# Attention passes of a graph network: each tile weighted right behind its scores, and each link of the scan chain in a turn of its own

## The chip, the core and the metric

The program runs on one NeuronCore of a Trainium2 chip. Its engines are TensorE (PE; its weight loads are listed apart as PEld), VectorE (DVE), ScalarE (ACT), GpSimd (POOL) and SyncE (SP). Each has its own queue of instructions, works it off in order, and meets the others through semaphores. The metric is the device time of one execution in microseconds, lower is better.

## The reference

Four layers of a graph network on 3125 nodes of 256 features. Each layer has a graph part, a mixing part over all nodes and an MLP or a mixture of experts. Three of the graph parts and the gate of one mixture are attention over edges: for each edge a score per head from its source and target node, a softmax over the edges that end in the same node, and the weighted sum of the sources' values. The first layer's:

```python
scores = jnp.einsum('ehd,ehd->eh', Q[dst], K[src]) * SCALE
attn_max = jnp.zeros((n, H), scores.dtype).at[dst].max(scores)
w = jnp.exp(scores - attn_max[dst])
attn_sum = jnp.zeros((n, H), w.dtype).at[dst].add(w)
w = w / (attn_sum[dst] + 1e-08)
msg = V[src] * w[:, :, None]
out = jnp.zeros((n, H, D), msg.dtype).at[dst].add(msg)
```

The third layer builds each edge's message from two rows with the edge's two attributes; the gate of the first mixture and the fourth layer add a number of the source to one of the target, and send the sum through a leaky ReLU. All of it is float32.

## The kernel before, in words

Edges are sorted by target node. A row of an edge tile holds up to 8 edges (SLOTS = 8) of one target, a tile has NP = 125 rows. `edge_pass` (L502) goes over the G tiles of a pass. It runs four times: "ae" (kind "dot", 8 heads, 125 tiles, a ring of 4 row buffers, of which one lies in `net_X`), "be" ("add", 4 heads, 91 tiles, ring of 8, the experts' matmuls as `inner`), "ee" ("mix", 4 heads, 125 tiles, ring of 5, a mixing part as `beside`) and "ge" ("add", 8 heads, 125 tiles, ring of 5, nothing beside). For each tile g:

- POOL gathers 8 x 125 rows of the sources' table from HBM by indirect DMAs (L581), one for each slot, into place g mod RING of the ring. For the first slot it waits until the tile RING places back has been used: slot_summed of TensorE, in ee (for every slot) message_ready of DVE.
- ACT makes a one-hot matrix of the rows' targets (`one_hot`, L679, L681). TensorE turns it (`turn`, L608), ACT copies the turned one out of PSUM (`turned_copy`, L689), and TensorE looks up the target's own vector with it (`own`, L617). These three are missing in ee.
- DVE computes the scores (`score`, L740 to L768), the largest score of each row (`top`), and the scores less it (`below`). ACT takes the exponential (`weigh`, L695). DVE weights the gathered values with it (`send`, L778 in ee, L781 elsewhere) and sums the weights (L784).
- TensorE sums the 8 slots into PSUM with an identity matrix (`sum_slots`, L627). ACT copies the sum out (`keep`, L703).
- Every 4 tiles (a block b) follows the scan chain, which finds each node's maximum across rows: TensorE transposes the block's tops (`flip`, L638), DVE scans them forth and back (`scan`, L791, L796), TensorE transposes the result back (`flip_back`, L644, L645), DVE takes the differences (`fall_behind`, L809), ACT their exponentials (`factors`, L712 to L714), and DVE lowers what has been gathered so far (`lower`, L816).
- DVE scales the kept sum by its factor (`scale`, L824), TensorE adds the rows of one node together with the one-hot matrix (`total`, L652), and DVE adds that to the accumulator (`add`, L830).

The order on each engine is written out by hand: each engine runs a loop over turns i, and in a turn does one step for each of several tiles, as for DVE `score(i + 1)`, `send(i)`, `scale(i - 6)`, `add(i - 7)`. PSUM holds two tiles of sums: `sum_slots(g)` waits for `keep` of g - 2. There is one buffer for the weights (`weigh(g)` waits for `send(g - 1)`) and one for the totals (`total(g)` waits for `add(g - 1)`).

`sum_pass` (L856), between be and ee, gathers tiles in the same way with a ring of 4, but has no scores: TensorE sums the slots as they arrive.

## Time and profile before

| | |
|---|---|
| median of 3 runs | 12751.7 us (12729.91 to 12787.16) |
| profiled execution, span | 12797.9 us, mean granted TensorE clock 0.722 |
| TensorE matmul busy | 7767.2 us, 61% |
| VectorE busy | 6057.8 us, 47% |
| GpSimd busy | 6028.7 us, 47% |
| ScalarE busy | 2346.5 us, 18% |
| gathers and scatters of GpSimd | 621.62 MB, 22.6% of the 16 DMA engines' time |

No time of the profiled execution is known but its span from the first to the last instruction; it is 46 us above the median of the runs. Busy is the time in which an engine has an instruction under way. The idle time of an engine is listed with what ended it: "issue" when the profile shows nothing that it waited for, "remote" when a semaphore ended it whose sender the profile doesn't name. Semaphores are used again by later stages, so a releaser's name can be that of another stage.

### The profile page before, as it was taken

The numbers are of one execution on the slowest core, as the hardware profiler recorded it, in microseconds if no ns is written. First come the engines' busy times: TensorE is split into PE (matmuls) and PEld (weight loads), VectorE is DVE, ScalarE is ACT, GpSimd is POOL, SyncE is SP. The second block draws the span as 40 slices with busy tenths as digits, with TensorE's granted clock in tenths as the row PEclk, the third lists the DMA queues.
The fourth block names the chain that finished last, engine by engine and source line by source line (L and its number), as shares of the span: only waits on it lengthen the run. The fifth ranks groups of instructions, "written<-read, shape, count | busy, mean of one in ns | idle before, by whom it ended". The sixth has DMA issues, their size and how long they took to land. (4 is left out here: it accounts for less than half of the span.)

```text
span 12797.9 us, 114013 instructions
## 1 busy us (share of the span) xinstructions
PE 7767.2 (61%) x32472; PEld 6013.2 (47%) x32472; DVE 6057.8 (47%) x17050; ACT 2346.5 (18%) x5596; POOL 6028.7 (47%) x6164
## 2 busy tenths in 40 slices
PE   4555365256665468844777675676646846666546
PEld 3433344245554367743566433455535635554334
DVE  6556565378886322222122144665551134444455
ACT  0111001011110134420122011133311211111001
POOL 0666546566663066614666504665521136666000
PEclk9655555577777677767788786777768967777777
DMA  1212122166665111222333601121343323336200
GB/s 46 60 58 61 42 75 65 46 175 184 183 183 111 27 17 19 19 52 80 92 91 92 77 7 47 45 45 42 40 43 101 105 58 96 95 95 90 32 4 22
DMA packets 478286, 903.72 MB, mean 71 GB/s; under 512 B 173139, under 2 KB 290029, under 8 KB 476915
## 3 DMA queue, kind: packets, MB, share of 16 engines
q0 software_dynamic: 277568, 621.62, 22.6%
q1 hardware_dynamic: 200106, 274.86, 6.7%
q8 instruction: 271, 4.44, 0.1%
q14 instruction: 341, 2.79, 0.1%
HBM read 827.17 MB, written 68.88 MB: 70 GB/s over the span
## 5 line engine op out<-in xcount | busy, mean ns | idle before, releaser
L581 POOL DMA_INDIRECT ee_rows<-e_table,net_mr_data x1000 | 999.7, 1000 | 1097.9 <-POOLq L1725 468.0
L581 POOL DMA_INDIRECT ge_rows<-g_table,net_mr_data x1000 | 961.0, 961 | 654.0 <-issue 285.7
L913 POOL DMA_INDIRECT ce_rows<-c_table,net_mr_data x1000 | 947.7, 948 | 501.0 <-issue 246.0
L402 POOL DMA_INDIRECT main_slots<-em_load,em_where x784 | 807.8, 1030 | 690.1 <-DVE em_where L376 439.3
L581 POOL DMA_INDIRECT ae_rows<-a_table,net_mr_data x752 | 719.2, 956 | 431.9 <-issue 216.4
L581 POOL DMA_INDIRECT be_rows<-b_table,bx_br_data x728 | 696.3, 957 | 454.9 <-issue 196.6
L627 PE MATMUL ee_to_act<-ee_message,net_eye 125*125 125x256 f32 x2000 | 599.0, 447 | 211.9 <-issue 208.3
L627 PE MATMUL ge_to_act<-ge_rows,net_eye 125*125 125x256 f32 x2000 | 633.7, 470 | 153.6 <-issue 145.7
L402 POOL DMA_INDIRECT gat_slots<-eg_load,eg_where x512 | 528.9, 1033 | 392.2 <-DVE eg_where L376 227.7
L936 PE MATMUL ce_part_ps<-ce_rows,net_eye 125*125 125x256 f32 x2000 | 577.2, 435 | 217.7 <-issue 111.5
L359 PE MATMUL em_look_ps<-em_table,em_hot_tT 25*128 25x125 f32 x1568 | 332.3, 391 | 565.9 <-issue 467.8
L627 PEld LDWEIGHTS ge_to_act<-ge_rows,net_eye 125*125 125x125 f32 x2000 | 466.2, 238 | 289.3 <-issue 201.1
L627 PEld LDWEIGHTS ee_to_act<-ee_message,net_eye 125*125 125x125 f32 x2000 | 439.4, 224 | 340.5 <-issue 266.0
L936 PEld LDWEIGHTS ce_part_ps<-ce_rows,net_eye 125*125 125x125 f32 x2000 | 425.3, 216 | 352.8 <-issue 180.0
L359 PEld LDWEIGHTS em_look_ps<-em_table,em_hot_tT 25*128 25x128 f32 x1568 | 307.6, 296 | 587.4 <-issue 497.2
L1101 DVE TENSOR_TENSOR c_acc<-c_acc,ce_total_ps 125x512 f32 x125 | 85.8, 686 | 858.6 <-remote 468.8
L359 PE MATMUL eg_look_ps<-eg_table,eg_hot_tT 25*128 25x125 f32 x1024 | 239.6, 421 | 387.1 <-issue 308.2
L652 PE MATMUL ae_total_ps<-ae_part,ae_hot 125*125 125x264 f32 x500 | 206.9, 554 | 400.8 <-issue 241.2
L2279 PE MATMUL be_own_h_bank<-bx_XT,bx_w 128*128 128x125 f32 x1600 | 311.9, 353 | 188.7 <-issue 114.0
L627 PE MATMUL ae_to_act<-ae_rows,net_eye 125*125 125x256 f32 x1504 | 412.2, 436 | 16.3 <-ACT ae_hotT L689 7.9
L359 PEld LDWEIGHTS eg_look_ps<-eg_table,eg_hot_tT 25*128 25x128 f32 x1024 | 222.9, 325 | 403.8 <-issue 383.0
L778 DVE TENSOR_TENSOR ee_message<-ee_rows,ee_weight 125x512 f32<-125x512 f32 x500 | 309.4, 680 | 181.8 <-remote 167.1
(1006 smaller groups left out, 18274.5 us busy)
## 6 DMA issues: line engine op xcount, KB each, us to landing
em_key_row<-main_keys SPq DMA_DIRECT2D x98, 512.0 KB
f_w<-in_L_ffn_W_dram SPq DMA_DIRECT2D x40, 1024.0 KB, 11.8
eg_key_row<-gat_keys SPq DMA_DIRECT2D x64, 512.0 KB
ce_rows<-c_table,net_mr_data POOLq DMA_INDIRECT x1000
ee_rows<-e_table,net_mr_data POOLq DMA_INDIRECT x1000
ge_rows<-g_table,net_mr_data POOLq DMA_INDIRECT x1000
main_slots<-em_load,em_where POOLq DMA_INDIRECT x784
b_own_rows<-bx_kept SPq DMA_DIRECT2D x100, 125.0 KB
```

The costliest lines, as they stand in the source:

```text
L359: ins = pe.matmul(look_ps[i % 2][:, u, 0:NP], hot_tT[:, i % 2, u * 128:(u + 1) * 128], table[:, i % 2, u, 0:NP], start=True, stop=True)
L402: pool.indirect_dma_start(edge["slots"], bass.IndirectOffsetOnAxis(ap=where[:, c:c + 1], axis=0), load[:, c, :], None).then_inc(scattered, 16)
L581: pool.indirect_dma_start(rows[n][:, s, :], None, table, bass.IndirectOffsetOnAxis(ap=data[:, g, s, 0:1].bitcast(I32), axis=0)).then_inc(g ...
L627: ins = pe.matmul(part_ps(g), const["eye"][0:NP, 0:NP], values(g)[:, s, :], start=(s == 0), stop=(s == SLOTS - 1))
L652: ins = pe.matmul(total_ps[0:NP, q, 0:WA], hot[0:NP, g % HOTS, q * NP:(q + 1) * NP], part[0:NP, g % PARTS, :], start=True, stop=True)
L778: ins = dve.tensor_tensor(message[0:NP, n, :, h * dv:(h + 1) * dv], r[0:NP, :, 0:dv], w[:, :, h:h + 1].to_broadcast([NP, SLOTS, dv]), ALU. ...
L913: pool.indirect_dma_start(rows[:, g % RING, s, :], None, table, bass.IndirectOffsetOnAxis(ap=data[:, g, s, 0:1].bitcast(I32), axis=0)).the ...
L936: pe.matmul(part_ps[g % 2][0:NP, 0:D], const["eye"][0:NP, 0:NP], rows[0:NP, g % RING, s, :], start=(s == 0), stop=(s == SLOTS - 1)).then_i ...
L1101: dve.tensor_tensor(at, at, total_ps[g % 2][0:NP, :, :], ALU.add).then_inc(added, 1)
L2279: ins = pe.matmul(self.h_bank[:, m * NP:(m + 1) * NP], self.w1[:, e, q, m * 128:(m + 1) * 128], self.XT[:, q, t * NP:(t + 1) * NP], start= ...
```

## The change

Only the order inside `edge_pass` is changed. On DVE a turn is now `score(i)`, `scale(i - 6)`, `send(i)`, `add(i - 7)`, `scan`; on TensorE `flip`, `flip_back`, `total(i - 7)`, `sum_slots(i)`, `turn(i + 4)`, `own(i + 2)`; on ACT `weigh(i)`, `keep(i - 1)`, `turned_copy(i + 3)`, `factors`, `one_hot(i + 5)`. The scan chain of block b is flip and scan in turn 4b + 4 (3 before), flip_back and fall_behind in 4b + 5 (4 and 5 before), lower in 4b + 7 (6 before). The waits that order the use of PSUM follow the new distances. The lines of the kernel from L834 on move down by one.

```diff
@@ def sum_slots(g) on TensorE
-                    if QW and g + 4 < G:
-                        pe.wait_ge(turned_sb, g + 5)
+                    if QW and g + 2 < G:
+                        pe.wait_ge(turned_sb, g + 3)
@@ TensorE's loop
-                for i in range(-5, G + 8):
+                for i in range(-6, G + 8):
+                    for b in range(BLOCKS):
+                        if i == b * BLOCK + 4:
+                            flip(b)
+                        if i == b * BLOCK + 5:
+                            flip_back(b)
                     if 0 <= i - 7 < G:
                         total(i - 7)
-                    for b in range(BLOCKS):
-                        if i == b * BLOCK + 3:
-                            flip(b)
-                        if i == b * BLOCK + 4:
-                            flip_back(b)
-                    if 0 <= i - 1 < G:
-                        sum_slots(i - 1)
-                    if QW and 0 <= i + 5 < G:
-                        turn(i + 5)
-                    if QW and 0 <= i + 3 < G:
-                        own(i + 3)
+                    if 0 <= i < G:
+                        sum_slots(i)
+                    if QW and 0 <= i + 4 < G:
+                        turn(i + 4)
+                    if QW and 0 <= i + 2 < G:
+                        own(i + 2)
@@ def turned_copy(g), def keep(g) on ACT
-                    if 0 <= g - 6 < G:
-                        act.wait_ge(slot_summed, g - 5)
+                    if 0 <= g - 4 < G:
+                        act.wait_ge(slot_summed, g - 3)
...
-                    if QW and g + 6 < G:
-                        act.wait_ge(turned, g + 7)
+                    if QW and g + 4 < G:
+                        act.wait_ge(turned, g + 5)
@@ ACT's loop
-                    if 0 <= i + 1 < G:
-                        weigh(i + 1)
-                    if QW and 0 <= i + 4 < G:
-                        turned_copy(i + 4)
-                    if 0 <= i - 2 < G:
-                        keep(i - 2)
+                    if 0 <= i < G:
+                        weigh(i)
+                    if 0 <= i - 1 < G:
+                        keep(i - 1)
+                    if QW and 0 <= i + 3 < G:
+                        turned_copy(i + 3)
...
-                    if 0 <= i + 6 < G:
-                        one_hot(i + 6)
+                    if 0 <= i + 5 < G:
+                        one_hot(i + 5)
                     if beside is not None:
-                        beside.scalar(act, i)
+                        beside.scalar(act, i - 1)
                     if inner is not None:
-                        inner.scalar(act, i)
+                        inner.scalar(act, i - 1)
@@ DVE's loop
-                    if 0 <= i + 1 < G:
-                        score(i + 1)
                     if 0 <= i < G:
-                        send(i)
+                        score(i)
...
                     if 0 <= i - 6 < G:
                         scale(i - 6)
+                    if 0 <= i < G:
+                        send(i)
+                    for b in range(BLOCKS):
+                        if i == b * BLOCK + 7:
+                            lower(b)
                     if 0 <= i - 7 < G:
                         add(i - 7)
                     for b in range(BLOCKS):
-                        if i == b * BLOCK + 6:
-                            lower(b)
-                        if i == b * BLOCK + 3:
+                        if i == b * BLOCK + 4:
                             scan(b)
```

DVE in ge, a turn that ends with a scan, before (the names are tiles and buffers; `ge_below` is what ACT's exponential reads, `ge_weight` what it writes):

```order
L749 TENSOR_TENSOR ge_term<-ge_rows,ge_own_ps 125x64
L760 SCALAR_TENSOR_TENSOR ge_raised<-ge_term 125x64
L762 TENSOR_TENSOR ge_raised<-ge_raised,net_mr_data 125x64
L764 TENSOR_REDUCE ge_row_top<-ge_raised 125x8
L766 TENSOR_SCALAR ge_top<-ge_row_top 125x8
L768 TENSOR_TENSOR ge_below<-ge_raised,ge_top 125x64
L781 TENSOR_TENSOR ge_rows<-ge_rows,ge_weight 125x8x256
L784 TENSOR_REDUCE ge_part<-ge_weight 125x8
L824 TENSOR_TENSOR ge_part<-ge_part,ge_factor 125x264
```

and now:

```order
L749 TENSOR_TENSOR ge_term<-ge_rows,ge_own_ps 125x64
L760 SCALAR_TENSOR_TENSOR ge_raised<-ge_term 125x64
L762 TENSOR_TENSOR ge_raised<-ge_raised,net_mr_data 125x64
L764 TENSOR_REDUCE ge_row_top<-ge_raised 125x8
L766 TENSOR_SCALAR ge_top<-ge_row_top 125x8
L768 TENSOR_TENSOR ge_below<-ge_raised,ge_top 125x64
L824 TENSOR_TENSOR ge_part<-ge_part,ge_factor 125x264
L781 TENSOR_TENSOR ge_rows<-ge_rows,ge_weight 125x8x256
L784 TENSOR_REDUCE ge_part<-ge_weight 125x8
```

In the first piece the rows up to L768 are of tile i + 1 and L781, L784 of tile i; in the second both are of tile i. `scale` (L824) has gone in between.

TensorE in ge, around the turn with the flip, before (L652 is `total`, L638 `flip`, L627 `sum_slots`, L608 `turn`, L617 `own`):

```order
L617 MATMUL ge_own_ps<-g_s,ge_hotT 125x8
L652 MATMUL ge_total_ps<-ge_part,ge_hot 125x272 x2
L638 MATMUL ge_topT_ps<-net_eye,ge_top 8x125 x4
L627 MATMUL ge_to_act<-ge_rows,net_eye 125x256 x8
L608 MATMUL ge_to_act<-net_eye,ge_hot 125x125 x2
```

and now:

```order
L617 MATMUL ge_own_ps<-g_s,ge_hotT 125x8
L638 MATMUL ge_topT_ps<-net_eye,ge_top 8x125 x4
L652 MATMUL ge_total_ps<-ge_part,ge_hot 125x272 x2
L627 MATMUL ge_to_act<-ge_rows,net_eye 125x256 x8
L608 MATMUL ge_to_act<-net_eye,ge_hot 125x125 x2
```

The flip has gone ahead of the total. The sum is of tile i - 1 in the first piece and of tile i in the second, the turned tile i + 5 and i + 4, the looked-up tile i + 3 and i + 2.

## Rows read from the trace of the kernel before

**Rows 1.** Busy time of each stretch; columns as in its first line:

```profile
core 0: us, PE busy (x) PEld busy (x) DVE busy (x) ACT busy (x) POOL busy (x), PEclk, DMA share, GB/s
2573.00:4079.00 1506.00, 996.60 (x3563) 770.16 (x3564) 1209.80 (x1506) 220.38 (x690) 954.97 (x1000) 0.78 0.65 175
4450.00:5586.00 1136.00, 888.89 (x4909) 803.45 (x4910) 275.43 (x1182) 496.75 (x1164) 696.33 (x728) 0.73 0.17 19
...
7770.00:9443.00 1673.00, 1130.50 (x4212) 806.48 (x4213) 971.45 (x2307) 474.42 (x1140) 999.74 (x1000) 0.76 0.28 44
10436.00:11937.00 1501.00, 950.66 (x3564) 744.14 (x3564) 699.60 (x1507) 247.01 (x815) 960.99 (x1000) 0.73 0.43 91
```

**Rows 2.** POOL's waits by pass: engine, line, releaser, us in total, times, longest:

```profile
POOL ae_rows L581 <- remote: 116.1, 37, 5.5
POOL net_X L581 <- remote: 55.4, 17, 4.0
...
POOL be_rows L581 <- remote: 158.4, 81, 2.9
...
POOL ce_rows L913 <- remote: 124.0, 71, 4.5
POOL ce_rows L913 <- PE ce_part_ps L936: 114.2, 129, 4.4
...
POOL ee_rows L581 <- DVE ee_part L784: 333.5, 44, 14.9
...
POOL ge_rows L581 <- remote: 183.1, 60, 4.6
```

**Rows 3.** DVE's waits in ae, ge and ee:

```profile
DVE ae_rows L740 <- DMA ae_rows<-a_table,net_mr_data: 94.2, 41, 13.0
...
DVE a_acc L830 <- remote: 18.3, 13, 2.9
...
DVE g_acc L830 <- DMA eg_src_i<-in_gat_src_dram: 463.5, 90, 11.5
...
DVE ge_upto L791 <- remote: 86.8, 27, 5.3
...
DVE e_acc L830 <- remote: 339.8, 30, 21.6
```

**Rows 4.** Timeline of ge: start, us, engine, line, operation, count, [idle before, releaser]:

```profile
11031.21 0.50 PE L617 MATMUL ge_own_ps<-g_s,ge_hotT 125*125 x4
...
11034.32 1.79 PE L652 MATMUL ge_total_ps<-ge_part,ge_hot 125*125 125x272 f32 x4 [2.61 <-DVE g_acc L830]
...
11035.91 2.98 PE L627 MATMUL ge_to_act<-ge_rows,net_eye 125*125 125x256 f32 x8
...
11040.96 0.95 POOL L581 DMA_INDIRECT ge_rows<-g_table,net_mr_data  x1 [0.30 <-issue]
...
11044.59 1.87 PE L627 MATMUL ge_to_act<-ge_rows,net_eye 125*125 125x256 f32 x4 [1.51 <-issue]
...
11044.88 0.37 ACT L689 COPY ge_hotT<-ge_to_act 125x250 f32<-125x250 f32 x1 [6.30 <-remote]
11044.94 0.94 POOL L581 DMA_INDIRECT ge_rows<-g_table,net_mr_data  x1 [3.03 <-remote]
11044.97 0.72 DVE L830 TENSOR_TENSOR g_acc<-g_acc,ge_total_ps 125x544 f32 x1 [6.38 <-DMA eg_src_i<-in_gat_src_dram]
```

**Rows 5.** Timeline of ee, DVE and POOL:

```profile
8723.59 0.70 DVE L830 TENSOR_TENSOR e_acc<-e_acc,ee_total_ps 125x528 f32 x1 [16.18 <-remote]
...
8732.09 0.94 POOL L581 DMA_INDIRECT ee_rows<-e_table,net_mr_data  x1 [12.62 <-DVE ee_part L784]
```

**Rows 6.** Instructions on ge_rows: line, engine, count, ns min/median/max, first and last start:

```profile
L581 POOL DMA_INDIRECT ge_rows<-g_table,net_mr_data x1000: 940/946/1812, 10436.7 to 11872.0; - x167
...
L781 DVE TENSOR_TENSOR ge_rows<-ge_rows,ge_weight x125: 2269/2280/2289, 10459.9 to 11909.2; 125x2048 f32<-125x2048 f32 x125
```

**Rows 7.** Groups of ee from 7900 to 9300: count, busy us, mean ns, idle before:

```profile
L695 ACT ACT_TABLE_LOAD x46 | 59.0, 1283 | 73.2 <-issue 53.1 <-DVE ee_part L784 19.8
```

## The prediction

> **What bounds the kernel now.** I read the busy times by stretch first, then who waited for whom in each stretch, then a few microseconds of the timeline. The change touches only edge_pass, so the question is what holds its four runs: "ae" (2573 to 4079), "be" (4450 to 5586), "ee" (7770 to 9443) and "ge" (10436 to 11937), together 1506 + 1136 + 1673 + 1501 = 5816 us. The reader should see that no engine fills any of them: in ge TensorE's matmuls are busy 951 us of 1501, DVE 700, GpSimd (POOL) 961; in ae DVE 1210 of 1506 [rows 1]. The stretch 5870 to 7350 is sum_pass, which the diff leaves alone.
>
> A tile is 8 gathers of POOL. Where POOL is free to go on they start 1.25 us apart, 0.95 busy and 0.30 "issue" [rows 4], so 10.0 us a tile is a floor. The 1000 gathers of ge start over 1435.3 us, 11.5 us a tile [rows 6]; ae, with as many and a pass as long, is taken for the same [rows 1]. What lies between is POOL's wait for a free row buffer: 116.1 + 55.4 = 171.5 us in ae, 158.4 in be, 333.5 in ee, 183.1 in ge, in all 846.5 us [rows 2]. That is the most that a better order can take out, 6.6% of the run.
>
> Why does POOL wait? In ae, be and ge for slot_summed, TensorE's sum of the tile 4, 8 or 5 places back; in ee for message_ready of DVE. DVE in turn waits 463.5 us in ge (90 times) at L830 for a total of TensorE (the releaser's name there, an input load of another stage, is that of a reused semaphore), and 339.8 us in ee at L830; in ae it waits 94.2 us for gathers at L740, and at L830 only 18.3 [rows 3]. So ae looks bound by the ring's round trip, ge and ee by TensorE's answers.
>
> The timeline shows something about those answers. In ge the lookup of 11031.21 is over by its record at 11031.71, but ACT's copy L689, which needs it, starts at 11044.88, after 6.30 us idle: 13.2 us late. The total of 11034.32 is over by its record at 11036.1, and DVE's add starts at 11044.97, after 6.38 us idle: 8.9 us late. POOL, waiting for the sum before that, starts at 11044.94, 3.03 us after it had stopped [rows 4]. Three engines come free within 0.09 us. In ee DVE's add, idle for 16.18 us, starts at 8723.59, in the middle of a pause of POOL of 12.62 us that ends at 8732.09 [rows 5], so 4.1 us after POOL fell silent (8732.09 - 12.62 = 8719.47). So beside a running stream of gathers TensorE's signals come late, and they come in a bunch 3 to 4 us after POOL stops. I infer that from these two places; no row names the cause.
>
> One control speaks loudly: sum_pass has no scores, no weights and no link of DVE ahead of its sums, and sums a tile as soon as it is there. Its ring has 4 places. POOL still waits 124.0 + 114.2 = 238 us in it [rows 2], 1.9 us a tile. A round trip without any DVE link buys no freedom from the wait.
>
> **The change, part by part.** No arithmetic is added or removed; each tile keeps its 16 sum, 4 total, 4 lookup and 2 turn matmul records, and 2.5 of flip and flip_back on average: 28.5.
>
> *Score and send in one turn.* Before, DVE scores tile i+1 and then weights tile i; now it scores and weights tile i. The sum of a tile comes one turn sooner after its gathers, so the ring gets about one turn (10 to 12 us) of slack. POOL's queue is not reordered, and each gather waits for the same sum. The gain is between 0 and the stalls. In ae DVE's busy time, 1210/125 = 9.7 us a tile, leaves POOL's 10.0 as the next floor, so all 171.5 us could go at most. I take 0 in all four: in sum_pass more slack than this left the wait where it is, and ge, whose DVE is busy for less than half of the pass, has the same time a tile as ae. What these two share with ae is TensorE's late answers.
>
> *The exp between them.* ACT's weigh (L695) now stands between score and send, with DVE's `scale` of another tile placed over it. In ee an ACT_TABLE_LOAD of 1.283 us comes ahead of it, 46 times in 1400 us [rows 7], which at 13.4 us a tile are 105 tiles; it starts right behind ACT's earlier work, since only the last wait is attached to the activation, and DVE's scores cover it (three operations over 544 values and five small ones): 0. If that cover is gone (ACT late in its turn) it costs up to 1.283 x 46/105 x 125 = 70 us in ee and, were every tile of be to load too, 1.283 x 91 = 117 there.
>
> *Flip, scan, flip back.* Flip stands ahead of the total now, and it and flip_back come a turn later. DVE's scan no longer waits after its add for four more records, 86.8 us in ge [rows 3]; but the total, and with it the add, is queued behind the flip. The same records precede the scan, so I take 0, with bounds of -87 and +87.
>
> *Work beside.* ACT's share of `beside` and `inner` moves by one turn with weigh and so keeps its place; TensorE's, DVE's and SP's keep theirs. 0.
>
> *Tail.* After the last gather lands, the send of the tile before and an add (2.28 + 0.72 = 3.0 us in ge [rows 4, 6], taken for ae and ee too, and for be at most that) no longer stand between its score and its send: 9 to 12 us gained, I take 12. Sum: 12797.9 - 12 = 12786 for the profiled execution. Its span is 46 us above the median of the three runs (12751.7), so the forecast is 12751.7 - 12 = 12740.
>
> The Trainium skill, "TensorE: Matmul & The Clock Gate", section "Architectural detail: the array is 16× 32×32, not 1× 128×128", gives TensorE a queue of 64 instructions, against 8 on the others. By it, with a weight load beside each matmul, some 32 records can be pending, hardly more than one tile's 28.5, so a longer ring would let no more be answered at each pause of POOL: the same forecast, while a ring that alone decided gives the first rival's time. The trace fits it: of the sum that starts at 11035.91 eight records go out in 2.98 us, and its next ones only as the answers come, up to 11044.6 [rows 4].
>
> **The rivals.**
> Faster: the ring decides, and one turn of slack removes the stalls where DVE has room. For: in ae DVE hardly waits for TensorE [rows 3], and its sums, being late because DVE is, would be asked for a whole turn after they are put in. Against: sum_pass. Price: ae 150 of its 171.5 us, half of ge's 183.1, a tenth of ee's 333.5 (there POOL waits for message_ready, and after the pause DVE still needs the 8.5 us from 8723.59 to 8732.09 for add, score and send, in either order [rows 5]), nothing in be, whose ring of 8 is the longest and which still stalls for 81 of its 728/8 = 91 tiles [rows 1, 2]: 150 + 92 + 33 = 275, so 12740 - 275 = 12465; half of it gives 12600.
>
> Slower: the lookup (own) becomes the late link. Before, score(i) found a lookup that had been queued three turns back; now own(i) is queued behind sum(i-2), which leaves only after send(i-2), and score(i) is due one turn after that. Place: L740 and L749. It decides once an answer is late by more than a turn less the sum and lookup themselves, 11.5 - 4 - 1 = 6.5 us (in [rows 4] eight of a sum's records take 3 us, a lookup 0.5; I take 4 and 1); [rows 4] shows 8.9 and 13.2. Price: in ae, where DVE has 11.5 - 9.7 = 1.8 us to spare a tile, a lateness of 10 at every second tile costs (10 - 6.5 - 1.8)/2 = 0.85 us a tile, one of 13.2 costs 2.45: 106 to 306 us; in ee the add now waits behind the sum with the score undone, up to 3.5 us at each of 30 waits [rows 3, 5], 105 us. I price it at 100 + 60 = 160: 12740 + 160 = 12900.
>
> That the change doesn't do what it says (the sums are written earlier but go out no earlier, since `part_kept(g-1)` and `turned_sb` hold them to the same tile as before) is the forecast's own mechanism.
>
> **How the numbers follow.** Forecast 0.38, with its own range 12690 to 12800; faster rival 0.31, slower rival 0.31. A measurement of this kernel can tell 0.5%, 64 us, from no change. Of the forecast's 0.38, 0.03 falls below 12688 and 0.02 above 12815; of each rival 0.01 falls within these. Faster 0.33, same 0.35, slower 0.32. The range is to hold 8 in 10: 12520 leaves out the fuller form of the faster rival, 12920 that of the slower.
>
> **What would show it.** Right: tile times of ae and ge stay at 11.4 to 11.8 us, POOL's waits at L581 sum to within 150 us of 846, and the add at L830 still waits in ge. The faster rival: POOL's waits in ae and ge under half, DVE's gather waits at L740 gone. The slower one: new idle time at L740 or L749 that TensorE's L617 ends, not a DMA. Wrong in any case: idle time of DVE ahead of L781 or L778 that ACT's L695 ends, over 50 us in ae or ge; or a sum_pass changed by more than 20 us, since nothing in it is touched.

## The result: slower by 0.9%, and the profile after

| | before | after |
|---|---|---|
| median, us | 12769.4 (4 runs) | 12872.2 (4 runs, 12868.92 to 12925.2) |
| profiled execution, span, us | 12797.9 | 12867.2 |

The ratio of after to before is 1.0086, 95% interval 1.0066 to 1.0106. The time lies in the range that was given, but not at the forecast of 12740, "no change". In us the medians are 103 apart, the two profiled executions 69.

The busy times by stretch of the changed kernel, columns as in [rows 1]:

```profile
2565.00:4100.00 1535.00, 972.37 (x3564) 756.31 (x3564) 1208.96 (x1506) 225.89 (x690) 965.23 (x1000) 0.78 0.64 172
4471.00:5640.00 1169.00, 928.98 (x4994) 832.86 (x4994) 271.38 (x1195) 515.88 (x1177) 701.14 (x728) 0.73 0.16 18
5903.00:7373.00 1470.00, 1020.32 (x4150) 801.68 (x4150) 245.11 (x728) 219.86 (x473) 949.61 (x1000) 0.80 0.40 92
7797.00:9499.00 1702.00, 1115.29 (x4230) 812.85 (x4230) 980.52 (x2319) 476.86 (x1143) 1003.21 (x1000) 0.77 0.27 43
10481.00:12008.00 1527.00, 952.24 (x3564) 733.91 (x3564) 698.69 (x1507) 252.22 (x815) 970.22 (x1000) 0.72 0.43 90
```

Measured from the first to the last instruction of a pass (for be and ee the windows of [rows 1] are some 20 and 11 us shorter than that), ae went from 1507 to 1535 us, be from 1157 to 1168, ee from 1683 to 1703, ge from 1501 to 1526: 84 us more. ce, sum_pass, which the diff leaves alone, took 1471 and 1470. No engine has more instructions, and the granted clock of each stretch is within 0.01 of the one in [rows 1], so neither explains the 84 us.

Counted along POOL, from the start of its first gather of a pass to the pass's last instruction, they come apart like this. The result's pair is one execution of each kernel; b0 is the changed kernel once more (below):

| us over ae, be, ee and ge | before | after | more | more in b0 |
|---|---|---|---|---|
| gathers busy | 3612 | 3640 | 28 | 13 |
| pauses of POOL with a releaser | 920 | 938 | 18 | 69 |
| pauses called "issue" | 1065 | 1061 | -4 | -4 |
| from the last gather's end to the pass's end | 251 | 293 | 42 | 45 |

So half of the loss in this pair is a longer tail of the passes, and it is the same in b0. The gathers got longer where DVE weights: those whose middle falls in L781 took 0.986 us on average in ge and 0.963 in ae (0.945 and 0.946 before), in ee at L778 0.985 (0.944). Why is not shown; `scale` now stands directly ahead of that step.

DVE's and POOL's waits, as in [rows 2, 3]; the names of ae, ee and ge in turn:

```profile
DVE a_acc L830 <- remote: 141.0, 46, 10.4
DVE ae_gap L809 <- remote: 31.9, 5, 9.7
...
DVE e_acc L830 <- remote: 387.8, 34, 23.1
...
DVE ee_gap L809 <- remote: 48.1, 12, 6.4
...
DVE g_acc L830 <- DMA eg_src_i<-in_gat_src_dram: 581.6, 58, 22.4
...
DVE ge_term L749 <- PE ge_own_ps L617: 2.4, 1, 2.4
...
POOL ee_rows L581 <- DVE ee_part L784: 334.1, 55, 16.1
...
POOL ge_rows L581 <- remote: 134.7, 43, 4.4
POOL ge_rows L581 <- PE ge_to_act L627: 77.7, 20, 7.9
```

DVE in ae used to wait for gathers [rows 3]; now it waits for totals (18.3 us before, 141.0 now). In ge POOL now waits 77.7 us in 20 waits for a sum that TensorE is still doing by its records; before that was 6.4 us in two, while its waits named "remote" were 183.1 us and are 134.7 now.

A second reading shows what the waits are made of. A total of ge, the add that needs it, and the gather that starts beside it (timeline: start, us, engine, line, operation, count, [idle before, releaser]):

```profile
11361.65 1.08 PE L652 MATMUL ge_total_ps<-ge_part,ge_hot 125*125 125x272 f32 x4
...
11369.05 0.34 PE L608 MATMUL ge_to_act<-net_eye,ge_hot 125*125 125x125 f32 x1 [1.06 <-issue]
11371.82 0.17 PE L617 MATMUL ge_own_ps<-g_s,ge_hotT 125*125 x1 [2.43 <-issue]
...
11383.23 0.72 DVE L830 TENSOR_TENSOR g_acc<-g_acc,ge_total_ps 125x544 f32 x1 [22.38 <-DMA eg_src_i<-in_gat_src_dram]
...
11383.52 0.95 POOL L581 DMA_INDIRECT ge_rows<-g_table,net_mr_data  x1 [4.15 <-remote]
```

The total is over by its record at 11362.73, and DVE, idle for 22.38 us, gets it at 11383.23. POOL had gathered for three tiles without a pause and then stopped for 4.15 us. The answer comes 3.9 us into that stop. It is what [rows 4] showed, with a longer delay. TensorE's own next records also thin out while POOL gathers: from 11366.21 to 11374.64 they start 0.7 to 2.8 us apart, with "issue" ahead of them. The ends of TensorE's records are modelled, so these rows don't tell whether the matmul itself is late or only its answer; "late" means late by the record.

In ee one of POOL's long pauses, in the changed kernel:

```profile
8734.27 0.70 DVE L830 TENSOR_TENSOR e_acc<-e_acc,ee_total_ps 125x528 f32 x1 [15.83 <-remote]
...
8730.09 0.95 POOL L581 DMA_INDIRECT ee_rows<-e_table,net_mr_data  x1 [0.30 <-issue]
8742.33 0.95 POOL L581 DMA_INDIRECT ee_rows<-e_table,net_mr_data  x1 [11.29 <-DVE ee_part L784]
```

From the add (8734.27) to the next gather (8742.33) it takes 8.1 us, against the 8.5 read from [rows 5]. Coming back after the answer takes what it did. POOL pauses more often, 55 times against 44, but in this pair the pauses are shorter and sum to the same, 334.1 and 333.5 us: here ee's 20 us more are its tail (72 us in place of 54). In b0 they sum to 370.3.

### The profile page after: what moved, and what is told of

The parts are those of the page before. It is cut to its first block and busy times, and to the rows that moved or that the text cites. A ratio compares the mean times of both kernels' runs of the same rounds, so it can differ in the third digit from the quotient of the medians.

```text
span 12867.2 us, 114013 instructions
## 1 busy us (share of the span) xinstructions
PE 7696.0 (60%) x32472; PEld 5977.0 (46%) x32472; DVE 6058.9 (47%) x17050; ACT 2377.0 (18%) x5596; POOL 6068.4 (47%) x6164
## 5 line engine op out<-in xcount | busy, mean ns | idle before, releaser
L627 PE MATMUL ee_to_act<-ee_message,net_eye 125*125 125x256 f32 x2000 | 612.7, 468 | 372.0 <-DVE ee_part L784 275.1
L627 PE MATMUL ge_to_act<-ge_rows,net_eye 125*125 125x256 f32 x2000 | 639.8, 478 | 247.2 <-issue 145.8
L627 PE MATMUL ae_to_act<-ae_rows,net_eye 125*125 125x256 f32 x1504 | 495.2, 501 | 386.6 <-DVE ae_part L784 196.8
L627 PEld LDWEIGHTS ee_to_act<-ee_message,net_eye 125*125 125x125 f32 x2000 | 465.0, 238 | 518.1 <-DVE ee_part L784 310.5
L627 PEld LDWEIGHTS ge_to_act<-ge_rows,net_eye 125*125 125x125 f32 x2000 | 473.6, 242 | 409.6 <-issue 192.5
L937 PE MATMUL ce_part_ps<-ce_rows,net_eye 125*125 125x256 f32 x2000 | 542.7, 420 | 179.1 <-DMA ce_rows<-c_table,net_mr_data 98.6
L627 PEld LDWEIGHTS ae_to_act<-ae_rows,net_eye 125*125 125x125 f32 x1504 | 376.6, 257 | 507.6 <-issue 214.6
L830 DVE TENSOR_TENSOR g_acc<-g_acc,ge_total_ps 125x544 f32 x125 | 89.9, 719 | 658.1 <-DMA eg_src_i<-in_gat_src_dram 581.6
## 6 DMA issues: line engine op xcount, KB each, us to landing
f_w<-in_L_ffn_W_dram SPq DMA_DIRECT2D x40, 1024.0 KB, 11.7
```

The source lines that it names most:

```text
L627: ins = pe.matmul(part_ps(g), const["eye"][0:NP, 0:NP], values(g)[:, s, :], start=(s == 0), stop=(s == SLOTS - 1))
L830: dve.tensor_tensor(at, at, total_ps[0:NP, :, 0:WA], ALU.add).then_inc(added, 1)
L937: pe.matmul(part_ps[g % 2][0:NP, 0:D], const["eye"][0:NP, 0:NP], rows[0:NP, g % RING, s, :], start=(s == 0), stop=(s == SLOTS - 1)).then_i ...
```

## The experiments

Every ratio is to the kernel before, run in the same set on the same chip; kernels of different sets are compared by ratio only. Spans of ee are of the one profiled execution. The chips differ: sum_pass, which no run touches, takes 1480 to 1484 us in the first and the third set and 1469 to 1472 in the others, so a span in us is compared within its set, or with a set of the same kind. Sets: a1 to a4; b0, m1, m2, v1; c1, c2, d2, d1; h1, g1, w3, w4; k1, w5. The medians of the kernel before were 12853, 12781, 12867, 12776 and 12777 us.

| run | what | ratio, 95% interval | ee, us | POOL's waits in ee, us, times |
|---|---|---|---|---|
| a1 | pairing alone | 1.0079 (1.0063 to 1.0095) | 1780 | 422.2, 54 |
| a2 | chain alone | 0.9991 (0.9980 to 1.0002) | 1659 | 293.2, 45 |
| a3 | fall_behind behind send | 1.0095 (1.0078 to 1.0113) | 1771 | 411.5, 56 |
| a4 | total ahead of flip | 1.0112 (1.0096 to 1.0129) | 1776 | 429.6, 56 |
| b0 | the changed kernel | 1.0063 (1.0040 to 1.0086) | 1730 | 370.3, 53 |
| c1 | change in ee alone | 1.0071 (1.0052 to 1.0089) | 1776 | 406.6, 52 |
| c2 | change in all but ee | 1.0026 (1.0010 to 1.0041) | 1678 | 326.4, 50 |
| d1 | add a tile later | 1.0112 (1.0087 to 1.0136) | 1781 | 401.5, 63 |
| d2 | score and weigh paired | 1.0205 (1.0184 to 1.0225) | 1725 | 379.3, 52 |
| h1 | score paired, nothing else | 1.0027 (1.0014 to 1.0039) | 1687 | 321.7, 45 |
| g1 | pairing, beside first | 1.0082 (1.0066 to 1.0098) | 1791 | 444.9, 64 |
| k1 | changed, keep later | 1.0086 (1.0065 to 1.0107) | 1724 | 359.5, 54 |
| w3 | DVE sums be, ee, ge | 1.0159 (1.0143 to 1.0176) | 1584 | 181.3, 38 |
| w4 | the same, changed order | 1.0249 (1.0229 to 1.0269) | 1717 | 319.6, 56 |
| w5 | DVE sums ee alone | 0.9914 (0.9899 to 0.9929) | 1589 | 192.9, 42 |

### Which half of the change

The diffs from here on leave out context and some of the `if` lines.

a1_pair_only, from the changed kernel:

```diff
+                        total(i - 7)                    # TensorE
-                        if i == b * BLOCK + 4:
+                        if i == b * BLOCK + 3:
                             flip(b)
-                        if i == b * BLOCK + 5:
+                        if i == b * BLOCK + 4:
                             flip_back(b)
-                        total(i - 7)
                         sum_slots(i)
                         score(i)                        # DVE
+                        send(i)
                             fall_behind(b)
                         scale(i - 6)
-                        send(i)
-                            lower(b)                    # 4b + 7
                         add(i - 7)
+                            lower(b)                    # 4b + 6
-                        if i == b * BLOCK + 4:
+                        if i == b * BLOCK + 3:
                             scan(b)
```

> The pairing alone: score(i), send(i), sum_slots(i), turn(i + 4), own(i + 2) as in the changed kernel, but the scan chain in the turns it had before (flip and scan 4b + 3 behind total, flip_back 4b + 4, fall_behind 4b + 5 behind send, lower 4b + 6). Theory C (the chain costs: fall_behind now stands between score and send and waits there for a late flip_back, 36 us in ae, 105 in be, 54 in ee, 4 in ge by the waits at L809): the loss is gone, 12740 to 12800. Theory P (the pairing costs: DVE scores a tile later, and its add at the end of a turn holds the next score, so POOL comes to wait for a sum that is really under way, 20 times and 77.7 us in ge): the loss stays, 12850 to 12900.

a2_chain_only, from the kernel before:

```diff
-                        total(i - 7)                    # TensorE
-                        if i == b * BLOCK + 3:
+                        if i == b * BLOCK + 4:
                             flip(b)
-                        if i == b * BLOCK + 4:
+                        if i == b * BLOCK + 5:
                             flip_back(b)
+                        total(i - 7)
                         sum_slots(i - 1)
                         score(i + 1)                    # DVE, then as in the changed kernel
```

> The chain alone: the kernel before with score(i + 1), send(i), sum_slots(i - 1) kept, and flip, flip_back ahead of total and a turn later, fall_behind and scale ahead of send, lower ahead of add in 4b + 7. Theory C: 12850 to 12900, with new idle time of DVE at L809. Theory P: 12750 to 12790, as before.

a3_fall_last, from the changed kernel, on DVE:

```diff
-                        if i == b * BLOCK + 5:
-                            fall_behind(b)
                     if 0 <= i - 6 < G:
                         scale(i - 6)
                     if 0 <= i < G:
                         send(i)
+                        if i == b * BLOCK + 5:
+                            fall_behind(b)
```

> The changed kernel with one step moved: fall_behind(b) behind send(i) instead of between score(i) and send(i). Theory C: the waits at L809 no longer hold a send, and half or more of the loss comes back, 12770 to 12820. Theory P: within 25 us of the changed kernel, 12850 to 12900.

a4_total_first: `total(i - 7)` moved ahead of flip and flip_back, nothing else.

> The changed kernel with TensorE's total(i - 7) ahead of flip and flip_back, as before. Theory T (the add is late because its total stands behind flip and flip_back): ge, where the add waits longest (581.6 us at L830 against 463.5), gets its 25 us back, and ae a part: 12820 to 12845. Theories C and P: no change against the changed kernel, within 20 us.

The pairing costs, the moved chain does not (1.0079 and 0.9991), as theory P wanted. The waits at L809 were real. In ae of the changed kernel:

```profile
3367.14 0.19 DVE L809 TENSOR_TENSOR ae_gap<-net_X,ae_topT_ps 125x32 f32<-125x32 f32 x1 [9.69 <-remote]
...
3367.59 2.28 DVE L781 TENSOR_TENSOR ae_rows<-ae_rows,ae_weight 125x2048 f32<-125x2048 f32 x1
...
3377.04 0.95 POOL L581 DMA_INDIRECT ae_rows<-a_table,net_mr_data  x1 [11.41 <-PE ae_to_act L627]
```

A send (L781) is held for 9.69 us and POOL for 11.41. But a3, which has them behind the send, gains nothing (1.0095). Theory C falls. So does T: a4 is no faster (1.0112).

### Which pass, and is it TensorE

b0_changed_again is the changed kernel unchanged.

> The changed kernel once more, on the chip of the other runs of this call. The pairing alone has been seen to cost 0.8% and the chain nothing. Theory E (it costs in ee, where TensorE's total now follows directly on a sum that waits for the last send, and beside's matmuls stand there too): ee is 60 to 120 us longer than in the kernel before, ae and ge together less than 40. Theory P (DVE a tile later in every pass): all of ae, ge and ee by 20 to 40 us each. Ratio 1.006 to 1.010 in both.

Its ratio is 1.0063. ae takes 1540, ee 1730 and ge 1533 us, 33, 47 and 32 more than before. That is nearly what theory P wanted (20 to 40 in each) and not what theory E did (60 to 120 in ee, less than 40 in ae and ge together).

c1 and c2 take the whole change if `kind == "mix"`, and if not.

> The whole change in ee alone; ae, be and ge keep the order of before. Theory E (the pairing costs in ee above all, since there TensorE also has beside's matmuls between a sum and the next total): ratio to before 1.004 to 1.009. Theory P (it costs in every pass alike): 1.001 to 1.003.

> The whole change in ae, be and ge; ee keeps the order of before. Theory E: 1.000 to 1.004. Theory P: 1.005 to 1.008. With c1_ee_alone it should add up to the changed kernel's 1.0063 to 1.0086.

0.71% lies in ee and 0.26% in the three other passes together: both lie in theory E's ranges and outside P's. The sum, 0.97%, meets the 0.86% of the changed kernel and is a little over the 0.63% of b0. In this set ee takes 1776 us in c1 and 1679 in c2. Of the 97 us 80 are POOL's waits (406.6 and 326.4) and 18 the tail. But the same code of ee took 20 and 47 us more than before in the profiles of the result's pair and of b0. That ee loses is seen in each; how much of the loss is ee's differs from set to set, and theory E's reason for it, the mixing part's matmuls, is not shown by c1 and c2.

m1_half_sum and m2_half_gather bear on the late answers. Both leave work out: m1 half of each tile's sum, m2 half of its gathers:

```diff
-                    for s in range(SLOTS):                            # sum_slots, m1
+                    for s in range(SLOTS // 2):
-                    for s in range(SLOTS):                            # POOL, m2
+                    for s in range(SLOTS if g < RING else SLOTS // 2):
```

> The kernel before with 4 of the 8 slots summed in sum_slots of all four passes (the other 4 are left out of the sum): 8 matmul records a tile fewer, 20.5 instead of 28.5 in ae and ge. Theory R (TensorE's records come through only in the gaps between gathers, so a tile costs 8 x 0.95 us and a fixed share for each record, (11.5 - 7.6)/28.5 = 0.137 us): ae and ge fall to 10.4 us a tile, 135 us each, be by 50 to 100 us; 280 to 350 us faster in all. Theory Q (what counts is that POOL must pause for about 3 us for every second tile, however much stands behind it): ae and ge stay at 11.3 to 11.6 us a tile, within 60 us of the kernel before.

> The kernel before with 4 of the 8 gathers of a tile left out beyond the ring's first filling (slots 4 to 7 keep stale rows). Both R and Q (the lateness comes with the gathers): TensorE's signals come on time, the waits of the add at L830 in ge nearly go, and ge takes 7 to 8.5 us a tile, ae its 9.7 us of DVE. Rival M (TensorE itself is the bound at 11.5 us a tile, its records only show the dispatch): ae and ge stay near 11.5 us a tile.

m1's ratio is 0.9962 (0.9943 to 0.9981); ge with 1000 matmuls fewer takes 1489 us. Theory R, a price for each record, wanted 135 us there and falls; theory Q's range holds (ae takes 1494 us). m2's ratio is 0.8700 (0.8676 to 0.8724), and ge takes 938 us, 7.5 a tile:

```profile
9328.00:10267.00 939.00, 776.67 (x3564) 649.74 (x3564) 689.94 (x1507) 242.04 (x815) 501.72 (x520) 0.86 0.35 77
```

The same 3564 matmuls fit into 939 us, so TensorE's work is not the bound at 1501 (rival M falls). DVE's waits at L830 in ge are 107.0 us in place of 463.5 [rows 3]. Late answers still occur there, but behind a pause of POOL they come at once:

```profile
9740.37 1.16 PE L652 MATMUL ge_total_ps<-ge_part,ge_hot 125*125 125x272 f32 x4
...
9741.68 0.72 DVE L830 TENSOR_TENSOR g_acc<-g_acc,ge_total_ps 125x544 f32 x1 [0.17 <-PE ge_total_ps L652]
...
9740.24 0.94 POOL L581 DMA_INDIRECT ge_rows<-g_table,net_mr_data  x1 [6.85 <-PE ge_to_act L627]
```

The total is over at 9741.53 and the add starts 0.15 us later. So the lateness goes with the gathers: where it is long, an unbroken row of them runs beside it, and with half of them most of it is gone. By what way they delay TensorE's answers no run shows.

### The theory of the fresh sum

d2_dve_paired: `score(i + 1)` and ACT's `weigh(i + 1)` of the kernel before made `score(i)` and `weigh(i)`.

> The kernel before with DVE's score(i + 1) made score(i) and ACT's weigh(i + 1) made weigh(i), and nothing else: DVE and ACT are paired as in the changed kernel, but TensorE keeps its turns, so total(i - 7) stands behind sum_slots(i - 2), which has been ready for a turn, instead of behind sum_slots(i - 1), which waits for the last send. Theory S (what costs is that the total, and with it the add that DVE waits for, is queued directly behind a sum that is only just asked for): the loss is gone, 0.998 to 1.002. Theory D (what costs is that DVE scores a tile later, with its add ahead of the next score): the loss stays, 1.006 to 1.010.

d1_add_later, from the changed kernel, on DVE:

```diff
                         score(i)
+                        lower(b)                # in turn 4b + 8
+                        add(i - 8)
                         scale(i - 6)
                         send(i)
-                        add(i - 7)
```

> The changed kernel with DVE's add a tile later and between score and send: score(i), add(i - 8), scale(i - 6), send(i), and lower(b) ahead of the add in turn 4b + 8. The total that an add needs has then all of send(i - 1) and score(i) to come back, and is not behind sum_slots(i - 1) any more. Theory S: the waits at L830 fall in ee and ge and the loss is gone or more, 0.994 to 1.002. Theory D: 1.005 to 1.012, since every send now stands behind an add that waits.

d2 moved more than it was to: weigh(i) now stands behind ACT's share of the turn before.

```profile
DVE be_rows L781 <- ACT be_weight L695: 927.6, 91, 11.8
...
DVE ee_message L778 <- ACT ee_weight L695: 483.6, 89, 25.0
...
DVE e_acc L830 <- remote: 28.2, 10, 8.3
```

be took 1417 us against 1174 and 1185 in c1 and c2, and the ratio, 1.0205, lies outside both ranges. It decides nothing on S or D, but shows that an exp left behind such work is dear. d1 is the clean one. In ee, first c1's wait for the total (c1 has the changed kernel's ee, in the same set), then d1's waits:

```profile
DVE e_acc L836 <- remote: 480.7, 39, 21.2
...
DVE e_acc L830 <- remote: 127.6, 18, 16.3
DVE ee_upto L791 <- DMA a_table<-em_d_out: 95.2, 11, 21.4
DVE em_stats L2671 <- ACT em_kv L2607: 93.6, 12, 17.6
DVE net_X L2688 <- ACT em_out L2635: 72.5, 5, 19.3
```

The wait for the total is down by 353 us, as theory S wanted, and the ratio is 1.0112; ee takes 1781 us against 1776. DVE waits instead for the flip, and for the mixing part. Theory S falls: the largest wait was where DVE noticed the lateness. The ratio lies in theory D's range.

### Score alone, beside's place, keep's place

h1_score_only, from the kernel before:

```diff
-                    if 0 <= i + 1 < G:
-                        score(i + 1)
+                    if 0 <= i < G:
+                        score(i)
```

> The kernel before with DVE's score(i + 1) made score(i) and nothing else: TensorE and ACT keep their order word for word, so sums, beside's matmuls and totals keep their distances. Theory H (the handshake costs: in the pairing TensorE waits for a send, 220.8 us at L627 in ee against 0 in its list before, and DVE then waits for a total behind that sum): ee returns to the time of before, ratio 0.998 to 1.003. Theory D (the lost lead of DVE's scores costs by itself): 1.006 to 1.010. d2 moved weigh too, and its exp then stood behind ACT's work of the turn before, 483.6 us at L778.

g1_beside_first: a1 with `beside.tensor(pe, i)` ahead of `sum_slots(i)`.

> The pairing alone (as in the first call) with beside's matmuls ahead of sum_slots(i) on TensorE instead of behind it, so that they stand between the same two sums as before. Theory B (ee loses because beside's matmuls now stand behind a sum that waits for the last send, and the mixing part's own steps come late): 1.000 to 1.003. Theories H and D: 1.006 to 1.010.

h1 is paired on DVE exactly as a1 is, and loses 0.27% where a1 loses 0.79% (and g1 0.82% in h1's own set), inside theory H's range and outside D's. Its tails are 25 us longer than before (276 and 251), most of its 34 us, and its ee takes 1687 us in place of 1683. The rest of a1's loss comes only when TensorE and ACT are shifted with DVE. That is a difference between two orders and not a price for the shift: d2 adds only weigh to h1 and costs 2.05%. g1 shows that it isn't beside's place on TensorE. In ee, TensorE's waits at L627 of h1 and then of the changed kernel, and ACT's of the changed kernel:

```profile
PE ee_to_act L627 <- ACT ee_part L703: 102.3, 55, 4.3
PE ee_to_act L627 <- DVE ee_part L784: 49.7, 1, 49.7
```

```profile
PE ee_to_act L627 <- DVE ee_part L784: 275.1, 66, 50.1
...
ACT ee_part L703 <- remote: 168.6, 25, 37.1
```

After the change TensorE stands waiting for the send (66 times; once in h1, at the start of the pass), and ACT stands in keep for the sum's late answer. The second could be tried alone:

```diff
-                    if 0 <= i - 1 < G:
-                        keep(i - 1)
+                    if 0 <= i - 2 < G:
+                        keep(i - 2)
```

> The changed kernel with one step of ACT moved: keep(i - 2) instead of keep(i - 1), as far behind its sum as before; TensorE and DVE keep the changed order. Theory K (ACT stands in keep for the late answer of a sum that has only just been asked for, 199.4 + 50.2 + 45.9 us at L703 in ee and 425.6 + 158.0 in ge against 14.7 and 14.0 before; behind it wait one_hot, turned_copy, the exponentials and beside's share, which TensorE needs ahead of its next total): the waits at L703 fall under 60 us in each pass, and ee returns to within 30 us of the kernel before; ratio 0.999 to 1.004. Theory H in the form that TensorE's own order costs (the total behind a fresh sum): 1.006 to 1.010, with the waits at L830 as they are.

In k1 L703 is gone from the longest waits of ee and ge, and the ratio is 1.0086 all the same (ee 1724 us). In ge ACT waits 571.0 us at L689, the next step that needs TensorE:

```profile
ACT ge_hotT L689 <- remote: 571.0, 67, 25.6
```

Theory K falls too; the ratio lies in H's range.

### Taking TensorE's sum out of the loop

v1_fold, from the kernel before, in send, with `range(SLOTS // 2)` in sum_slots:

```diff
+                    dve.drain()
+                    m = values(g)
+                    dve.tensor_tensor(m[:, 0:SLOTS // 2, :], m[:, 0:SLOTS // 2, :], m[:, SLOTS // 2:SLOTS, :], ALU.add)
```

> The kernel before, where DVE adds slots 4 to 7 to slots 0 to 3 behind the weighting (one more operation over 125 x 1024 elements, about half of the 2.28 us of L781, so 1.15 us), and TensorE sums 4 slots. Nothing is left out. Theory R: ge 10.4 us a tile, ae held by DVE at 9.7 + 1.2 = 10.9, be shorter, in all 150 to 300 us faster than the kernel before. Theory Q: the same time or slower by DVE's added 1.2 us where it is on the path, 0 to 150 us slower.

Ratio 0.9960 (0.9941 to 0.9980), which misses both: R wanted 150 to 300 us less, Q nothing less. ge and ae hardly move (1494 and 1499 us), ee takes 1639 us against the 1730 of b0 in the same set and 1683 before.

w3_dve_sums goes on to the end, for every kind but "dot":

```diff
+                    dve.tensor_tensor(m[:, 0:4, :], m[:, 0:4, :], m[:, 4:8, :], ALU.add)
+                    dve.drain()
+                    dve.tensor_tensor(m[:, 0:2, :], m[:, 0:2, :], m[:, 2:4, :], ALU.add)
+                    dve.drain()
+                    dve.tensor_tensor(part[...], m[:, 0, :], m[:, 1, :], ALU.add)
 # sum_slots and keep left away; POOL waits for message_ready
```

> The kernel before, where in be, ee and ge DVE itself sums the 8 slots by three additions (over 4, 2 and 1 slots of values, in ge about 1.15 + 0.6 + 0.3 us and three drains, some 2.2 us a tile beside its 5.6) straight into part: no sum_slots, no keep, and POOL waits for DVE's message_ready in place of slot_summed. Nothing is left out. If late signals of TensorE are what POOL waits for, its waits in ge and be fall by half or more and a tile goes toward the 10.0 us of the gathers: ge 100 to 180 us, be 60 to 150 us shorter, ee between 100 shorter and 60 longer: ratio 0.975 to 0.990. If not, DVE's extra work makes it 1.00 to 1.02.

> The same in the changed kernel: with no sum of TensorE behind a send, the pairing has nothing to be queued behind. Theory H: w4 is at the time of w3 within 0.3% but for ae's 25 to 30 us. Theory D: w4 stays 0.6% or more behind w3.

> The kernel before with DVE summing the slots in ee alone (w3 without its part in be and ge, which got 210 and 60 us longer while ee got 100 us shorter). Nothing is left out. If passes add up: ee 80 to 100 us shorter, the rest as before, ratio 0.991 to 0.995, faster than both kernels. If ee's gain in w3 came from its surroundings: 0.998 to 1.002.

w3 misses what it was to show: with no TensorE in the ring POOL's waits don't fall by half in ge and be, and its ratio lies in the range of "if not". By pass: ee 1584 us, but be 1369 and ge 1562. In ge POOL waits 200.2 us for DVE in place of 189.5. In be it pauses 41 times instead of 81, for 373.8 us instead of 158.4, and DVE and ACT wait long for the totals and the mixture's own answers:

```profile
DVE b_acc L838 <- remote: 551.2, 39, 16.4
...
POOL be_rows L582 <- DVE be_part L791: 373.8, 41, 14.3
...
ACT L2308 <- remote: 608.9, 43, 16.4
```

w5 keeps ee's part only and is faster than both kernels, 12670.4 us median (6 runs, 12661.64 to 12682.32). Its ee:

```profile
7725.00:9314.00 1589.00, 757.56 (x2230) 496.17 (x2230) 1272.12 (x2694) 434.43 (x1018) 1040.62 (x1000) 0.60 0.29 46
```

DVE has 300 us more work there than in [rows 1] and the pass is 94 us shorter. No wait at L838 (the add) is among DVE's longest (10.9 us), and POOL's waits are down from 333.5 us to 192.9.

w4 against w3 (1.0249 and 1.0159) says that the changed order loses 0.9% even where TensorE sums nothing in be, ee and ge. That is theory D's range, and theory H's is missed. ee takes 1717 us against 1584, 133 more, ge 1584 against 1562, be 1310 against 1369. So a fresh sum in TensorE's queue isn't needed for the loss. More than that: in ee w4 has no sum on TensorE and no keep on ACT, and turn and own don't exist there. What is left of the change in ee is the pairing on DVE, the chain's new turns, and where `factors` stands in ACT's order. The first two cost next to nothing by themselves where TensorE sums (h1's ee 1687 against 1683; a2's 1659 against c2's 1679), so these moves don't add up. The waits in ee of w3, then of w4:

```profile
PE em_bank_b L2587 <- ACT em_wkv L2637: 66.9, 17, 10.8
...
PE em_bank_b L2588 <- ACT em_wkv L2638: 144.5, 23, 12.0
...
PE em_bank_b L2588 <- ACT em_wq L2630: 83.2, 16, 18.6
...
DVE e_acc L838 <- remote: 161.5, 19, 13.0
```

TensorE waits more for ACT's share of the mixing part, and DVE for totals.

## Why the prediction was wrong

- **No engine fills a pass; late answers hold it.** Right as far as tested: with half of the gathers left out (m2) most of the lateness goes.
- **No stall is taken out.** Right. POOL's waits of the kinds of [rows 2] sum to 770 us in the profile after against 846, but those that name TensorE's L627 belong to them too, and with them it is 938 us against 920.
- **"Score and send in one turn" put at 0, and at no less than 0.** This is the step that failed, together with the tail. I wrote "The gain is between 0 and the stalls" and let nothing below 0 into it. The pairing costs 0.79%, 100 us (a1), and the whole change 0.71% in ee alone (c1). In the result's pair POOL's waits grew by 18 us (69 in b0) and the gathers by 28 (13 in b0), for which the sum has no term. Most of the cost comes only with TensorE's and ACT's shift, which I took for a mere renumbering.
- **Flip, scan, flip back: 0.** Right, 0.9991 (a2). In trace the wait moved from L791 (86.8 us in ge [rows 3], 23.4 after) to the totals.
- **Tail: -12 us.** Wrong in sign and the largest single share of the result's pair: +42 us, +45 in b0. In ae the last gather ended at 4027.8 and the last add at 4080.5, 53 us; after at 4039.1 and 4101.1, 62 us. So counted, ee went from 54 to 72 us and be from 79 to 101, ge from 65 to 58. I had counted what no longer stands between the last tile's score and its send, and not how far behind the gathers DVE is when they end: it then has 3, 6 and 5 tiles of ae, be and ee still to score, in place of 2, 4 and 3 (ge 3 in both). What I took for slack of the ring had become a backlog of DVE.
- **Work beside: 0.** ACT's share does keep its place behind weigh. But weigh now waits for a score that DVE makes a turn later, while TensorE's and DVE's shares stay where they were. No run moves ACT's share alone.
- **The exp between score and send: 0.** Right where it was put. DVE's waits for it at L778 are 44.5 us in ee, 42.7 of them one wait.
- **The slower rival** had the sign (12900 against 12872), not the place. Waits for the lookup by name are 2.4 us at L749 in ge; with those named "remote", which may be others, 39.5 us in three waits against 7.3 before. Its second part, ee's add, is where the wait was seen, but d1 took that wait away without a gain. That 12872 lies in the range is owed to this rival's price, and no run shows its mechanism: luck.

The signs that were to show the forecast right all came: 11.8 and 11.7 us a tile in ae and ge, POOL's waits within 150 us of 846, the add still waiting in ge, sum_pass unchanged. None of them looks at the tails, and 150 us of freedom in the waits is more than the whole loss.

sum_pass was no control for ee. It has no link of DVE in its ring. In ee POOL waits for DVE, and DVE for whichever answer of TensorE comes last.

One reading of [rows 4] doesn't hold either. The records of that sum after its first eight don't all wait for the answers: two more start at 11039.69 and 11042.49, while POOL gathers and before the three answers near 11044.9.

**What stays open.** In ee POOL stops 52 to 64 times in the runs with the changed order or the pairing and TensorE's sums, against 44 to 50 in those with TensorE's old turns (52 in d2), for 6 to 8 us each on average. Keep (k1), beside's place on TensorE (g1), the wait for the total (d1) and the sum itself (w4) have each been tried, and none alone gives the loss back. That TensorE's queue as a whole is asked later can't be all of it: in w4's ee TensorE keeps all its turns but the chain's, and the loss is there. An obvious candidate is untested. ACT's share of the mixing part stands behind weigh, weigh behind DVE's later score, and TensorE's next total behind its own share of the mixing part, which waits for ACT's; w4's longer waits at L2588 point that way, h1, which has the same order there and loses 4 us in ee, against it. ACT's share ahead of weigh would be the run to make. So the sign and the tails are shown, and the cause of ee's longer pauses is open.

## What to carry to other kernels

Where several engines share late answers, the step with the largest wait is only where the lateness is noticed: here 353 us of waiting at one line were removed and the time stayed. A reordering that gives one queue slack takes lead from another, so put a price below zero on it, and count the end of each pass as well: how many tiles are still to do when the gathers are over. Removing an engine from the loop (DVE doing the sum, for 300 us of work more) gained what no order did, and it did so in one pass of three only (ee 94 us shorter; be and ge got 212 and 61 us longer).

## What the runs showed of the hardware

- The reader of a total of TensorE can start long after the total's end by its record: 20.5 us in ge (11362.73 to 11383.23) beside gathers 1.25 us apart, and 0.15 us right behind a pause of POOL of 6.85 us (m2). The Trainium skill, "TensorE: Matmul & The Clock Gate", section "The cost: per-tile semaphore tail", puts the tail of a matmul's semaphore at 25 ns and some nanoseconds more for each tile and some tens for each increment. The second case is near that. The first is off by a factor of hundreds, and there the measurement decides.
- Gathers get longer beside some of DVE's operations: 1000 gathers of ee took 999.7 us busy before [rows 1] and 1040.6 in w5, with DVE's busy time up from 971 to 1272. In w5 the 92 gathers whose middle falls in the first addition (L786, both inputs in SBUF) took 1.392 us on average and up to 1.99; the 204 in the product of L777, which reads its weights from PSUM, took 0.946. The Trainium skill, "GPSIMD Engine Reference", section "1. Specifications", names contention with VectorE instructions that have two SBUF inputs. For these two operations the trace agrees.
